# Decoder layer on one core: attention loads from SyncE's queue, tail halves interleaved, and pieces of the stretch between rows at other places

## The reference

```python
x = x + mamba(layernorm(x))            # W_in, conv of 4 taps, silu, W_x, W_dt, scan, gate, W_out
x = x + xattn(layernorm(x), ctx_1024)  # linear layers, softmax over 154 keys, linear
x = x + ffn(layernorm(x))              # rms norm, top 2 of 8 experts, clipped gelu-like gate

xp, z = jnp.split(x @ W_in, 2, axis=-1)
xc = _silu(_causal_depthwise_conv(xp, conv_w, conv_b))
Bm, Cm = jnp.split(xc @ W_x, 2, axis=-1)
dt = jax.nn.softplus(xc @ W_dt + b_dt)
h = exp(dt[:, :, None] * A[None]) * h + (dt * u)[:, :, None] * B[:, None, :]   # 16 states of 512 channels
y = (einsum('bds,bs->bd', h, C) + D * u) * _silu(z)

attn = softmax(einsum('bqf,bkf->bqk', q, k) * scale); out = _lin(einsum('bqk,bkf->bqf', attn, v) + q, oW, ob)

p1 = einsum('bsh,eoh->bseo', nf, mlp1_weight) + mlp1_bias
g = minimum(p1[..., 0::2], 7); lin = clip(p1[..., 1::2], -7, 7)
p2 = einsum('bsei,ehi->bseh', g * sigmoid(1.702 * g) * (lin + 1), mlp2_weight) + mlp2_bias
```

## Time and profile before

| | us |
|---|---|
| median of 3 runs | 1504.59 (1502.41 to 1505.41) |
| the profiled execution | 1504.71 |
| its span, first to last instruction | 1502.9 |
| VectorE busy | 1327.0 (88%) |
| TensorE busy | 1218.4 (81%) |
| ScalarE busy | 999.3 (66%) |
| GpSimd busy | 949.9 (63%) |

### The profile page before, as it was taken

How to read it: one execution, slowest core, us unless ns; L and a number is a source line. 1 busy time by engine, 2 the same in 40 slices (tenths; PEclk the granted TensorE clock), 3 DMA queues, 4 the chain that set the end, 5 groups by cost and what they waited for, 6 DMA issues and landing times. The chain is left out here.

```text
span 1502.9 us, 22669 instructions
## 1 busy us (share of the span) xinstructions
PE 1218.4 (81%) x6134; PEld 853.0 (57%) x6134; DVE 1327.0 (88%) x1744; ACT 999.3 (66%) x1475; POOL 949.9 (63%) x522
## 2 busy tenths in 40 slices
PE   5978887689788888899788888899677777786897
PEld 2446664575555555685555555586355455575565
DVE  5479999888999999988899999988999999974687
ACT  5755554447978878837877877837777777732654
POOL 1379998514799889614798988723598988731000
PEclk9989998699899999999799999999789989897799
DMA  8112231421222212422121222512111112210111
GB/s 258 65 63 57 84 95 32 142 85 59 71 56 71 74 59 91 157 71 80 50 78 56 83 65 70 175 46 80 47 60 47 59 57 62 89 57 29 57 57 56
DMA packets 88013, 114.54 MB, mean 76 GB/s; under 512 B 9964, under 2 KB 62965, under 8 KB 87934
## 3 DMA queue, kind: packets, MB, share of 16 engines
q1 hardware_dynamic: 83836, 110.86, 23.5%
q10 hardware_dynamic: 4098, 2.74, 0.6%
HBM read 88.85 MB, written 24.73 MB: 76 GB/s over the span
## 5 line engine op out<-in xcount | busy, mean ns | idle before, releaser
L1827 DVE TENSOR_TENSOR_SCAN work<-ps,work 128x1024 f32<-128x1024 f32 x192 | 438.1, 2283 | 27.0 <-ACT ps L1299 24.9
L2413 PE MATMUL ps<-ident,work 128*128 128x128 f32 x1536 | 296.1, 314 | 163.4 <-DVE stage L1875 56.0
L1299 ACT ACTIVATE ps<-dt,a_neg 128x1024 f32<-128x1024 f32 x256 | 284.9, 1116 | 124.8 <-DVE work L1827 81.4
L2413 PEld LDWEIGHTS ps<-ident,work 128*128 128x128 f32 x1536 | 187.0, 156 | 287.4 <-DVE stage L1875 113.3
L887 POOL TENSOR_TENSOR work<-dtu,b_bc 128x1024 f32<-128x1024 f32 x124 | 290.2, 2369 | 44.4 <-PE ps L2413 43.2
L1875 DVE SCALAR_TENSOR_TENSOR stage<-ps,c_tok,stage 128x512 f32<-128x512 f32 x360 | 254.4, 733 | 9.7 <-PE ps L2413 8.2
L2435 PE MATMUL ps<-w,work 128*128 (+1 forms) x1024 | 250.0, 389 | 2.8 <-DVE work L2009 2.0
L2435 PEld LDWEIGHTS ps<-w,work 128*128 128x128 f32 x1024 | 195.9, 196 | 40.4 <-issue 4.1
L2385 PE MATMUL ps<-nfT,w 128*128 128x512 bf16 x512 | 163.6, 415 | 26.0 <-DVE work L1945 14.6
L887 POOL TENSOR_TENSOR work<-dtu,w_out 128x1024 f32<-128x1024 f32 x64 | 149.3, 2353 | 40.4 <-PE ps L2413 40.4
L906 POOL TENSOR_TENSOR stage<-stage,work 128x512 f32<-128x512 f32 x120 | 150.2, 1275 | 37.8 <-ACT work L1322 37.8
(11 more groups left out here) (189 smaller groups left out, 1921.8 us busy)
## 6 DMA issues: line engine op xcount, KB each, us to landing
b_bc<-b_rows SPq DMA_DIRECT2D x32, 512.0 KB, 4.8
w_out<-b_rows SPq DMA_DIRECT2D x32, 512.0 KB, 4.5
wbc<-combine_rows SPq DMA_DIRECT2D x64, 256.0 KB, 4.0
work<-z_rows SPq DMA_DIRECT2D x8, 1024.0 KB, 7.6
dtu<-conv_rows SPq DMA_DIRECT2D x12, 512.0 KB, 6.3
conv_rows<-mix SPq DMA_DIRECT2D x20, 256.0 KB, 2.8
stage<-in_x SPq DMA_DIRECT2D x8, 512.0 KB, 5.5
z_rows<-mix SPq DMA_DIRECT2D x16, 256.0 KB, 2.8
```

Of the source, the lines that this page charges most:

```text
L1299: act.activation(decay_in(d, alone, opening), dt[:, d, :], ACT.Exp, scale=a_neg[:, bass.ds(it * 2 + (d * N + hf * (N // 2) + par), 1)]).th ...
L1827: dve.tensor_tensor_scan(h, decays, h, 0.0, ALU.mult, ALU.add).then_inc(scan_done, 1)
L2413: mm = pe.transpose(ps[:, a % HT_BANKS, d * P:(d + 1) * P], slot(par, d)[:, a * P:(a + 1) * P], ident[:, :])
```

## The change

Five things, in code that is otherwise the same.

1. The 16 loads of `w_fold` are issued by SyncE, behind its own 19 first loads, and no longer by ScalarE.
2. In the tail the halves are interleaved: TensorE transposes the attention input of half 0 ahead of the last `O`, two of the query products stand between the halves' scores, VectorE spreads its `norm_apply`, `divide` and `mean_square` among the tiles, ScalarE takes the experts' input of half 0 ahead of the squares of half 1, GpSimd follows that order.
3. In the stretch between, VectorE computes `expert_input` ahead of the step and the next row's second statistics behind `opening_scan(0)`, and GpSimd's `norm_scale` moves with them.
4. `ZL` 1 moves from between the two `N` to between the halves of `Y`, with its keeping and storing, and `bias(0)` moves ahead of `up(0, 0, 1, 0, 0)`.
5. ScalarE computes the loop's first decay ahead of `keep_z` (in stretch 3 ahead of `linear_in`), so that the loop's first turn is written out as a loop of its own.

```diff
-        between_jobs = (both("Y") + both("O") + tiles_of("T2", 0) + [("ZL", 0, 0)] +
+        between_jobs = (tiles_of("Y", 0) + [("ZL", 1, 0)] + tiles_of("Y", 1) + both("O") + tiles_of("T2", 0) + [("ZL", 0, 0)] +
...
-                        both("N")[0:2] + [("ZL", 1, 0)] + both("N")[2:4] + steps[4:5] + [("G", 0, 0)] + steps[5:] + [("TN", 0, 0), ("C", 0, 0)] +
+                        both("N") + steps[4:5] + [("G", 0, 0)] + steps[5:] + [("TN", 0, 0), ("C", 0, 0)] +
                         both("TN")[1:] + [("CT", 0, c) for c in halves])
 
-        alone_jobs = head + rows_in + attend + tail
+        alone_jobs = head[:-1] + tiles_of("T2", 0) + head[-1:] + tiles_of("Q", 0) + tiles_of("T2", 1) + tiles_of("Q", 1) + attend + tail
...
-        between_banks = {("ZL", 0, 0): 5, ("ZL", 1, 0): 7, **dict(zip(both("Y"), (4, 5, 3, 4, 1, 3, 0, 4))),
+        between_banks = {("ZL", 0, 0): 5, ("ZL", 1, 0): 5, **dict(zip(both("Y"), (4, 5, 3, 4, 1, 3, 0, 4))),
...
-                         ("C", 0, 0): 0, **dict(zip(both("TN"), (5, 3, 6, 7))), ("CT", 0, 0): 7, ("CT", 0, 1): 6}
+                         ("C", 0, 0): 0, **dict(zip(both("TN"), (5, 2, 6, 7))), ("CT", 0, 0): 7, ("CT", 0, 1): 6}
...
+            for dst, name in ((qwT, "qWT"), (cwT, "cWT"), (kwT, "kWT"), (vwT, "vWT"), (owT, "oWT")):
+                sp.dma_start(dst, t[name].rearrange("(k p) f -> p k f", p=P)).then_inc(w_fold, 16)
...
                 if left:
+                    store_left(1)
                     store_left(0)
...
                     load_b(b, 0, 0, 1)
                 if left:
-                    store_left(1)
...
-                    for n in (1, 2, 3):
-                        for c in halves:
-                            norm_scale(n, r, c)
+                    for c in halves:
+                        norm_scale(1, r, c)
+                    for c in halves:
+                        norm_scale(2, r, c)
+                        norm_scale(3, r, c)
...
                 norm_scale(3, r, 0)
+                norm_scale(3, r, 1)
                 step_input(ph, 0)
-                norm_scale(3, r, 1)
                 step_input(ph, 1)
                 pool.wait_ge(b_loaded[0], b * (2 * ITS) * 16 + 16)
                 first_product(b, 0)
                 if n_row is not None:
                     norm_scale(0, n_row, 0)
                 step_input(ph, 2)
+                if n_row is not None:
+                    norm_scale(0, n_row, 1)
                 step_input(ph, 3)
                 first_product(b, 1)
                 step_input(ph, 4)
                 step_input(ph, 5)
                 first_product(b, 2)
-                if n_row is not None:
-                    norm_scale(0, n_row, 1)
...
                         sum_squares(c)
-                    for c in halves:
                         experts_in(c)
...
                     act.preload_act_table(ACT.Exp)
+                    if r > 0:
+                        keep_left(1)
...
                     experts_in(0)
-                    if r > 0:
-                        keep_left(1)
...
+                    new.decay(0, 1, 0, 0, 1)
+                    if n_row is not None:
                         new.keep_z(0, 0, 1)
                     else:
                         new.linear_in(0, 0, 1, 1)
...
-                def body(hf, it, par, first):
+                def body(hf, it, par, first, decayed=False):
...
-                    decay(b, bp is None, hf, it, par, 0)
+                    if not decayed:
+                        decay(b, bp is None, hf, it, par, 0)
...
-                    turns(act, body, begun=True)
+                    for hf in range(2):
+                        if hf == 0:
+
+                            with act.Fori(1, 2) as it:
+                                for par in range(2):
+                                    body(hf, it, par, False, decayed=par == 0)
+                        else:
+                            for par in range(2):
+                                body(hf, 0, par, par == 0)
+                        with act.Fori(2 - hf, ITS) as it:
+                            for par in range(2):
+                                body(hf, it, par, False)
...
                     add_to_stream("O", 0)
                     ph.wait_taken(dve, ("O", TH - 1, 0))
                     norm_stats(ph, 1, xt, 0)
-                    add_to_stream("O", 1)
+                    add_tile("O", 4)
+                    add_tile("O", 5)
                     norm_apply(ph, 1, xt, xn_c, xn_c_ready, 0)
+                    add_tile("O", 6)
+                    add_tile("O", 7)
                     ph.wait_taken(dve, ("O", TT - 1, 0))
                     norm_stats(ph, 1, xt, 1)
                     score_max(0)
                     norm_apply(ph, 1, xt, xn_c, xn_c_ready, 1)
+                    divide(0)
                     score_max(1)
-                    divide(0)
                     divide(1)
                     add_to_stream("V", 0)
                     ph.wait_taken(dve, ("V", TH - 1, 0))
                     norm_stats(ph, 2, xt, 0)
-                    add_to_stream("V", 1)
+                    add_tile("V", 4)
                     norm_apply(ph, 2, xt, xc16, x16_ready, 0)
+                    add_tile("V", 5)
+                    add_tile("V", 6)
+                    mean_square(0)
+                    add_tile("V", 7)
                     ph.wait_taken(dve, ("V", TT - 1, 0))
                     norm_stats(ph, 2, xt, 1)
-                    mean_square(0)
+                    expert_input(0)
                     norm_apply(ph, 2, xt, xc16, x16_ready, 1)
-                    expert_input(0)
                     mean_square(1)
                     expert_input(1)
...
                     mean_square(0)
                     norm_apply(ph, 2, xt, xc16, x16_ready, 1)
+                    expert_input(0)
                     step(0)
-                    expert_input(0)
                     mean_square(1)
                     if n_row is not None:
                         norm_stats(ph, 0, xn_a, 0, n_row)
+                    expert_input(1)
                     step(1)
-                    expert_input(1)
                     step(2)
                     opening_scan(0)
+                    if n_row is not None:
+                        norm_stats(ph, 0, xn_a, 1, n_row)
                     step(3)
...
                     opening_scan(1)
-                    if n_row is not None:
-                        norm_stats(ph, 0, xn_a, 1, n_row)
                     step(6)
...
+                    if job == ("T2", 0, 1):
+                        query_out(ph, 0)
+                        query_out(ph, 1)
                     if job == ("PT", 0, 0):
-                        for a in range(TH):
-                            query_out(ph, a)
+                        query_out(ph, 2)
+                        query_out(ph, 3)
...
                 old.last_transposes((6, 7))
+                if r > 0:
+                    do(ph, "ZL", 1, 0)
...
                 do_all(ph, tiles_of("N", 0))
-                if r > 0:
-                    do(ph, "ZL", 1, 0)
                 do_all(ph, tiles_of("N", 1))
...
                 new.first_transposes((4, 5))
+
+                ph.wait_taken(pe, ("CT", 0, NH - 1))
+                new.bias(0)
                 new.up(0, 0, 1, 0, 0)
                 new.first_transposes((6, 7))
                 new.up(0, 0, 1, 0, 1)
-
-                ph.wait_taken(pe, ("CT", 0, NH - 1))
-                new.bias(0)
                 new.up(0, 0, 1, 1, 0)
```

27 lines of the change are left out of this document (12 added, 15 removed).

## The result

The changed kernel takes 1489.14 us (median of 4 runs, 1486.67 to 1491.1), the kernel before 1505.0 in the same comparison: ratio 0.989, 95% interval 0.9871 to 0.9909. That is 15.9 us faster, where 16.8 was forecast (1487.8). Its profiled execution has a span of 1489.3 us, 13.6 less than before.

What follows compares the result with a forecast made beforehand. VectorE, busy 88% of the span, was taken as the bound; time could come only where it or the engine ahead stands still. Start 4.6 + stretches 8.5 + tail 3.7 = 16.8 us off 1504.7; median forecast 1487.8, range 1483.5 to 1492.

Steps and rivals of the forecast that it cites:

- Start, 4.6: Start: without ScalarE's 16 issues the first tiles start at 10.2 in place of 14.82; 4.6 us, bounds 1 and 5.9.
- cover: Start: small loads must land before the W_in products, and SyncE must finish its longer list before the first z.
- Stretch, front end, 1.2, 1.4 and 1.8: Stretches 1 to 3: new VectorE order and left-over product's move end opening scans 1.2, 1.4, 1.8 us earlier.
- The lock: Two stretches: VectorE/GpSimd port lock; if route_scores' cast missed its gap, route about 1 us later each, sum 1489.9.
- Stretch, back end, 0.5, 2.5 and 1.3: Loop heads: bias products moved and decay ahead of keep_z save 0.5, 2.5 and 1.3 us in stretches 1, 2, 3.
- at half clock they stick out by 1.7: Gap ahead of up: four bias products fit at full clock (about 1.9), but at half clock (3.78) exceed it by 1.7.
- Tail, 3.7: Tail: interleaved halves bring expert_input(1) about 3.6 us earlier; 3.7 taken, bounds 1.5 and 10.
- about 2.1: Tail: of 5.7 us, about 2.1 given back as ScalarE keeps half 0's transposes before squaring half 1.
- Start nothing: Start rival: small loads or SyncE's list end the wait instead of ScalarE's issues; 1492.4, chance 0.11.
- stretches nothing: Stretches rival: GpSimd's first product and keep_z take over, so no gain there; 1496.3, chance 0.12.
- loop heads slower: Loop heads rival: jumps into new code cost 2.39 us each, 1495.0, chance 0.03; over 5.6 or other sign turn 0.04.
- Clock stays at full: Tail rival: TensorE's clock stays full through shorter idle stretches, 5 us more gained; 1482.8, chance 0.10.

Runs made afterwards that it cites:

- start_alone: The kernel before with the start alone changed (16 loads issued by SyncE): 1499.05 us, ratio 0.9945.
- seven_loads_on_act: The changed kernel with the first seven of the 16 loads issued by ScalarE again: 1489.55 us, ratio 0.9882.
- again: The changed kernel once more, unaltered: 1486.93 us against 1507.43 for the kernel before, ratio 0.986.
- changed_same_chip: The changed kernel unaltered, run for comparison with three others on one chip: 1487.52 us.
- front_alone: The kernel before with only the order of VectorE and GpSimd in the stretches changed: 1507.15 us against 1507.18, ratio 0.9998.
- squares_first: The changed kernel with both sums of squares ahead of the first experts_in on ScalarE in the tail: 1484.16 us, ratio 0.9846.
- tail_alone: The kernel before with the tail's edits alone: 1502.11 us, ratio 0.9968.

## Why the prediction was right, and where it was not

- **Sum.** 16.8 forecast; by the runs 15.9, and 20.5 and 18.0 in the two later comparisons; 13.6, 14.1 and 18.0 by the three profiles. That the first lies within 1 us of the forecast is in part luck: start and tail came out as forecast or better, the three stretches at 7.4, 4.8 and 5.9 in the profiles where 8.5 was forecast, and the loops, which the sum left out, moved by up to 3.7.
- **Start, 4.6.** Right: 4.5 to 5.4 at the first scan, 5.7 in start_alone. `norm_row` came at 9.35 rather than 10.2, and x landed 0.5 earlier; the "up to 1.3" that the prediction allowed for is real and measured 0.9. Neither cover failed: small loads landed in 6.4 at the median in place of 11.0, and SyncE was through at 31.9. Its 16 added issues took 8.4 us (23.47 to 31.87) in place of 12.5 on ScalarE (0.95 to 13.49). That long issues are those beside full DMA engines fits before: 12 of its 13 issues of over 1 us ran while the DMA share was over 1.0. It is not the whole of it, since the 16 on SyncE took 0.33 to 0.64 us each at shares of 1.08 and 1.12 up to 30 us. The rule of the Trainium skill ("DMA: Bandwidth & Descriptors", section "Issuing engines are not separate DMA queues") would have made the move worth next to nothing: start_alone has 8.3 by the runs. What the Trainium skill says there of the shared 16 engines fits beside that: in seven_loads_on_act x lands 0.5 us and `norm_row` comes 0.9 us later.
- **Stretch, front end, 1.2, 1.4 and 1.8.** The steps stood (2.16 of waiting ahead of `opening_scan(0)`, expert inputs at 1.13). The last opening scans came 1.0, 1.5 and 1.0 earlier in the first profile, so stretch 3 was put 0.8 too high. In row 1 again and changed_same_chip have them 0.1 and 0.2 us later than before: half clock fell on the transposes of `Y` and on the first scores, 1.1 to 1.2 us ahead of all opening scans. VectorE's and GpSimd's part of it showed no gain in the runs of front_alone; the prediction left out that a product at half clock can eat such a lead.
- **The lock** of the Trainium skill ("SBUF — State Buffer", section "Who interferes with whom"). The trace agrees: 1.13 in place of 2.14 and 4.25. The cast in `route_scores` did not miss its gap as that rival had it: 0.20 and 0.19 us in rows 1 and 2, where before had 2.07 and 2.32, and 1.72 in row 3, where before had 2.32. Another operation was held in rows 1 and 2, 1.83, with the opening scans as early as said above.
- **Stretch, back end, 0.5, 2.5 and 1.3.** Row 2: 3.5 at the loop's first scan, 3.0 from its second on. The step that was mis-sized is "at half clock they stick out by 1.7": in the gap the products never ran at half clock. Row 3: 1.4 at the first scan in all three profiles, of which again gives 1.1 back at the second. Row 1 is the term that failed: 1.7 forecast for the stretch, the table has -0.6, +0.7 and +0.8 (minus is a gain). Of this the back end, forecast to give 0.5, gave 0.5 at the first scan and cost 0.4, 0.6 and 0.6 at the second, for which TensorE's transposes stand behind `keep_z`. There before had full clock on bias and z and nothing to lose, and in the changed kernel the 16 z products meet half clock (3.14, 3.33 and 3.35 us in the three profiles, in place of 1.95). "The clock was full" was read from one execution and taken as the rule for this place; the rest of the miss is the front end's half clock above.
- **Tail, 3.7.** Right: 3.7 to 4.4 nearer to the first `O`. The give-back of "about 2.1" is shown by squares_first, which gets 1.4 to 2.1 of it back. The old tail stood at 47.0 to 50.0 us in five profiles, the new at 42.8 to 43.4 in seven, so the one profile of before was a good one, and the change is worth about 5 rather than 4 here (48.5 and 43.4 at the median); tail_alone has 5.3 by the runs.
- **Left out altogether**: that the loops, unchanged, would not pass in the same time. Row 3's took 1.5 to 3.7 longer in the changed kernel than in the one profile of before (1.2 to 3.5 longer in three kernels that have the old loop), and row 0's 0.9 longer to 1.6 shorter.
- **The rivals.** Start nothing, stretches nothing, loop heads slower (no first scan waits over 0.33 us): all fall. "Clock stays at full" in the tail falls as well: the row from 1370 has 0.50.
